# A state-space mixer's first step: loads in order of need, late step sizes, one chunk split on another engine

## The reference

```
proj = x @ W_in.T                       # 512 + 512 + 32*128 + 32*128 + 32 columns
val, gate, B, C, dt = split(proj)
val  = silu(depthwise_conv4(val) + conv_b)
ld   = softplus(dt + dt_bias) * -exp(A_log)
M    = (C . B per head) * exp(cum(ld)[l] - cum(ld)[m]), l >= m
Y    = M @ val + D * val
out  = (Y * silu(gate)) @ W_out.T
```

## Time and profile before

| what | value |
|---|---|
| median of 3 runs | 813.26 us (808.52 to 814.21) |
| profiled execution | 812.88 us, span 811.1 us |
| TensorE busy | 738.9 us, 91% |
| VectorE, ScalarE, GpSimd busy | 74%, 53%, 46% |
| mean granted TensorE clock | 0.965 of full speed |
| step 0 of the mixer ends, step 1 begins | 57.05 us |

### The profile page before, as it was taken

How to read it: one execution, slowest core, us unless ns; L and a number is a source line. 1 busy time by engine, 2 the same in 40 slices (tenths; PEclk the granted TensorE clock), 3 DMA queues, 4 the chain that set the end, 5 groups by cost and what they waited for, 6 DMA issues and landing times. The chain is left out here.

```text
span 811.1 us, 17004 instructions
## 1 busy us (share of the span) xinstructions
PE 738.9 (91%) x5786; PEld 401.0 (49%) x5791; DVE 598.5 (74%) x1037; ACT 432.8 (53%) x781; POOL 370.0 (46%) x408
## 2 busy tenths in 40 slices
PE   6699999999999999999999999997799998686673
PEld 2355565555655555555555565665134443333342
DVE  4578767687686786776767778885788898449995
ACT  5665445754444664544575544554277887532333
POOL 5466337463453583433749637633023212115672
PEclk9799999999999999999999999999699999798997
DMA  7355421227423132542223533220230000034401
GB/s 262 97 168 169 104 51 54 65 50 126 134 52 87 43 78 52 168 103 49 54 58 84 98 72 67 62 45 1 95 112 22 21 22 21 0 127 167 151 26 52
DMA packets 35509, 66.28 MB, mean 82 GB/s; under 512 B 7121, under 2 KB 12113, under 8 KB 33873
## 3 DMA queue, kind: packets, MB, share of 16 engines
q1 hardware_dynamic: 34896, 65.28, 30.0%
q10 hardware_dynamic: 576, 0.56, 0.2%
HBM read 62.49 MB, written 2.42 MB: 80 GB/s over the span
## 5 line engine op out<-in xcount | busy, mean ns | idle before, releaser
L280 POOL TENSOR_TENSOR cum_rows<-cum_rows,cum_t 128x512 f32<-128x512 f32 x128 | 136.4, 1076 | 195.4 <-DMA cum_rows<-cum_scratch 195.4
L758 PE MATMUL pring<-xt_hi,w_hi 128*128 (+1 forms) x576 | 173.5, 383 | 11.5 <-DVE conv_h L647 6.8
L758 PE MATMUL pring<-xt_lo,w_hi 128*128 (+1 forms) x576 | 172.8, 382 | 0.0
L758 PE MATMUL pring<-xt_hi,w_lo 128*128 (+1 forms) x576 | 172.7, 382 | 0.0
L626 DVE TENSOR_TENSOR bt<-pring,bt 128x512 f16<-128x512 f32 x128 | 88.1, 688 | 74.1 <-ACT bt L434 74.0
L434 ACT CAST bt<-pring 128x512 f16<-128x512 f32 x128 | 74.6, 583 | 116.8 <-PE pring L758 116.8
L630 DVE TENSOR_TENSOR ct<-pring,ct 128x512 f16<-128x512 f32 x128 | 88.2, 689 | 55.6 <-ACT ct L438 55.3
L797 PEld LDWEIGHTS pscore<-ct,bt 128*128 128x128 f16 x1536 | 95.9, 98 | 34.7 <-issue 7.2
L797 PE MATMUL pscore<-ct,bt 128*128 128x128 f16 x1536 | 106.7, 219 | 2.9 <-DVE mt L598 2.2
L438 ACT CAST ct<-pring 128x512 f16<-128x512 f32 x128 | 74.8, 584 | 54.8 <-PE pring L758 54.8
L1089 DVE TENSOR_REDUCE mx<-bank_at 128x4 f32<-128x512 f32 x128 | 83.5, 689 | 14.0 <-PE bank_at L1165 13.0
(11 more groups left out here) (154 smaller groups left out, 944.2 us busy)
## 6 DMA issues: line engine op xcount, KB each, us to landing
cum_rows<-cum_scratch SPq DMA_DIRECT2D x32, 1024.0 KB, 8.0
w_raw<-in_w_in SPq DMA_DIRECT2D x34, 256.0 KB, 7.1
weight_b<-weight_scratch SPq DMA_DIRECT2D x8, 1024.0 KB, 6.5
q_rows<-in_xt SPq DMA_DIRECT2D x4, 512.0 KB, 6.1
acc<-in_x SPq DMA_DIRECT2D x1, 2048.0 KB, 7.6
vals<-in_vals SPq DMA_DIRECT2D x16, 128.0 KB, 2.0
out<-acc SPq DMA_DIRECT2D x4, 512.0 KB, 2.9
w_raw_e<-in_w_up SPq DMA_DIRECT2D x1, 1024.0 KB, 4.8
```

The lines of the kernel that those rows point to most:

```text
L280: nc.gpsimd.tensor_tensor(rows[:, par, :, q], rows[:, par, :, q], own, ALU.subtract).then_inc(sem("since"), 1)
L758: mm = nc.tensor.matmul(bank[name][:], w[:, c, k, cols], x[:, k, bass.ds(n % TB, 1), :].rearrange("p o n -> p (o n)"), start=(i == 0), sto ...
```

## The change

The first step alone is reordered, on all engines; the arithmetic stays the same.

- **Loads.** SyncE issues x block 0, chunks 1 and 2, `ident`, chunk 3, x block 1, chunk 4; then it waits for the running sum of block 0, stores it, issues the two row loads, and behind these chunks 5 and 6, x block 2, chunks 7 and 8, x block 3, `dskip` and `wo`. The load of `acc` waits for the second row load, and the store of the other three sums comes behind it. ScalarE's queue has wdt, chunk 0, dtb, cw. `in_dtb` now counts dtb and cw, `in_wo` counts `dskip` and `wo`, and all waiters want both.
- **Chunk 0.** ScalarE makes only the high part; the low part is one VectorE operation.
- **Softplus** of blocks 1 to 3, and their dt products, go from before slot 0 to slot 4 (TensorE after `turn_values`, ScalarE after `evac_c(0, 4)`).
- **x's blocks.** Blocks 1 to 3 are split on GpSimd: block 1 between chunks 2 and 3, block 2 behind the eight exponents of step 0, block 3 behind those of step 1. TensorE's step 1 is taken out of the loop, and waits for blocks 2 and 3 stand behind it.
- **VectorE** computes the low part and the taps' scaling before the step sizes; the scaling of `dskip` stands behind `low_c(0, 1)`.

```diff
 @block.sync
-            for t in range(TB):
-                sp.dma_start(xt_raw[:, t], io["xt"][:, t]).then_inc(sem(f"in_xt{t}"), 16)
-            for t, name in ((cw, "cw"), (dskip, "dskip"), (ident, "ident")):
-                sp.dma_start(t[:], io[name]).then_inc(sem("in_early"), 16)
-            for c in range(2, CHUNKS):
-                load_chunk(c)
-            sp.dma_start(wo, io["wo"]).then_inc(sem("in_wo"), 16)
+            load_x(0)
+            load_chunk(1)
+            load_chunk(2)
+            sp.dma_start(ident[:], io["ident"]).then_inc(sem("in_ident"), 16)
+            load_chunk(3)
+            load_x(1)
+            load_chunk(4)
...
             for par in range(2):
                 load_rows(0, par, par)
+            load_chunk(5)
+            load_chunk(6)
+            load_x(2)
+            load_chunk(7)
+            load_chunk(8)
+            load_x(3)
+            sp.dma_start(dskip[:], io["dskip"]).then_inc(sem("in_wo"), 16)
+            sp.dma_start(wo, io["wo"]).then_inc(sem("in_wo"), 16)
+            sp.wait_ge(sem("rows1"), 16)
+            sp.dma_start(acc[:], io["x"]).then_inc(sem("in_x"), 16)
+            sp.dma_start(expo[:], io["expo"]).then_inc(sem("in_x"), 16)
             sp.wait_ge(sem("dt_cum"), TB)
             store_sums(1, TB)
-            sp.dma_start(acc[:], io["x"]).then_inc(sem("in_x"), 16)
-            sp.dma_start(expo[:], io["expo"]).then_inc(sem("in_x"), 16)
 @block.gpsimd
-            lo_part(0, 0)
+            pool.wait_ge(sem("w_ready"), 1)
             lo_part(0, 1)
-            split_x(2)
-            split_x(3)
             lo_part(0, 2)
+            split_x(1)
             lo_part(0, 3)
             lo_part(0, 4)
...
+            split_x(2)
+            pool.wait_ge(sem("cum_t"), 2)
             exponents(1, 0)
+            exponents(1, 1)
+            split_x(3)
 @block.scalar
             act.dma_start(wdt[:], io["wdt"]).then_inc(sem("in_wdt"), 16)
+            act.dma_start(w_raw[:, 0], io["w_in"][0, :, 0]).then_inc(chunk_loaded(0), 16)
             act.dma_start(dtb[:], io["dtb"]).then_inc(sem("in_dtb"), 16)
+            act.dma_start(cw[:], io["cw"]).then_inc(sem("in_dtb"), 16)
...
             split_x(0)
             hi_part(0, 0, True)
-            hi_part(0, 1, True)
+            act.wait_ge(sem("in_dtb"), 32)
+            nc.scalar.activation(rate[:, 0:1], dtb[:, 1:2], ACT.Exp).then_inc(sem("rate"), 1)
             act.wait_ge(sem("dt_mm"), 1)
             softplus(slice(0, L), 0)
-            split_x(1)
+            hi_part(0, 1, True)
             hi_part(0, 2, True)
...
+                tanh_gate(0)
+                evac_b(0, 0)
+                tanh_val(0)
+                hi_part(0, 3, True)
+                evac_c(0, 0)
+                hi_part(0, 4, True)
+                evac_b(0, 1)
+                evac_c(0, 1)
+                hi_part(0, 5, True)
+                evac_b(0, 2)
+                evac_c(0, 2)
+                decays(0, 0)
+                hi_part(0, 6, True)
...
+                evac_c(0, 4)
+                act.wait_ge(sem("dt_mm"), TB)
+                softplus(slice(L, TOK), 3)
+                evac_b(0, 5)
+                hi_part(0, 8, True)
+                evac_c(0, 5)
+                decays(0, 4)
 @block.vector
             split_x(0)
+            dve.wait_ge(sem("w_hi"), 1)
+            nc.vector.scalar_tensor_tensor(out=w_lo[:, 0], in0=w_raw[:, 0], scalar=W_SCALE, in1=w_hi[:, 0], op0=ALU.mult, op1=ALU.subtract).then_inc(sem("w_ready"), 1)
+            dve.wait_ge(sem("in_dtb"), 32)
...
                 low_c(0, 1)
+                dve.wait_ge(sem("in_wo"), 32)
+                nc.vector.tensor_scalar(dskip[:], dskip[:], W_SCALE * W_SCALE, None, ALU.mult).then_inc(sem("cw_half"), 1)
                 low_b(0, 2)
 @block.tensor
...
                 scores(0, 2)
                 turn_values(0)
+                for t in range(1, TB):
+                    step_widths(t)
                 for s in range(4, SLOTS):
```

More of the change, by code:

```diff
@@ L324, in refill @@
                     lo_part(g + 1, c)
-            with pool.Fori(1, TB - 1) as n:
-                exponents(n, 1)
-                exponents(n + 1, 0)
             refill(0)
@@ L397, in hi_part @@
                         act.wait_ge(sem("c_proj"), (TB * g - 1) * SLOTS + c)
+                if first and c == 0:
+                    nc.scalar.mul(w_hi[:, c], w_raw[:, c], W_SCALE).then_inc(sem("w_hi"), 1)
+                    return
                 nc.scalar.mul(w_hi[:, c], w_raw[:, c], W_SCALE)
                 nc.scalar.mul(w_raw[:, c], w_raw[:, c], W_SCALE).then_inc(sem("w_hi"), 1)
-            act.wait_ge(sem("in_dtb"), 16)
-            nc.scalar.activation(rate[:, 0:1], dtb[:, 1:2], ACT.Exp).then_inc(sem("rate"), 1)
             def softplus(s, done):
@@ L452, in first_step @@
             def first_step():
[L454 to L460, removed]
+                tanh_gate(0)
[11 more added lines that the diff above has]
+                hi_part(0, 6, True)
                 evac_b(0, 3)
-                decays(0, 0)
+                decays(0, 1)
                 evac_c(0, 3)
-                decays(0, 1)
-                hi_part(0, 6, True)
                 decays(0, 2)
+                hi_part(0, 7, True)
                 evac_b(0, 4)
@@ L469, in first_step @@
                 evac_c(0, 4)
-                hi_part(0, 7, True)
+                act.wait_ge(sem("dt_mm"), TB)
[3 more added lines that the diff above has]
+                evac_c(0, 5)
                 decays(0, 4)
-                evac_b(0, 5)
-                evac_c(0, 5)
+                evac_b(0, 6)
                 decays(0, 5)
[L475 to L480, removed]
+                evac_c(0, 6)
+                decays(0, 6)
+                act.wait_ge(sem("in_wo"), 32)
                 nc.scalar.copy(wo_parts[:, 0], wo).then_inc(sem("wo_hi"), 1)
+                evac_b(0, 7)
+                evac_c(0, 7)
+                decays(0, 7)
             def step(n, refill=None, queries=()):
-                silus(n)
+                tanh_gate(n)
+                tanh_val(n)
                 if refill is not None:
@@ L581, in _ @@
             sums(0)
[L582 to L586, removed]
+            dve.wait_ge(sem("cw_half"), 2)
             dve.wait_ge(sem("zeroed"), 1)
@@ L688, in first_step @@
                 low_c(0, 3)
-                sums(3)
                 weigh(0, 2)
                 pad_values(0)
[L692 to L697, removed]
+                low_b(0, 4)
+                low_c(0, 4)
+                weigh(0, 3)
+                step_sizes(slice(L, TOK), 3)
+                low_b(0, 5)
+                rates(slice(L, TOK), 3)
+                sums(1)
+                sums(2)
+                sums(3)
+                low_c(0, 5)
+                weigh(0, 4)
+                low_b(0, 6)
+                low_c(0, 6)
+                weigh(0, 5)
+                low_b(0, 7)
+                low_c(0, 7)
+                weigh(0, 6)
+                sums_turned(1, TB)
+                dve.wait_ge(sem("cw_half"), 3)
             def step(n, norm=False):
@@ L765, in warm, with step_widths @@
                                  start=True, stop=True)
[L767 to L771, removed]
+            def step_widths(t):
                 pe.wait_ge(sem(f"in_xt{t}"), 16)
@@ L888, in _ @@
             first_step()
-            with pe.Fori(1, STEPS - 2) as n:
+            step(1)
+            pe.wait_ge(sem("xt_late"), 6)
+            with pe.Fori(2, STEPS - 2) as n:
                 step(n)
```

46 lines of the change are left out of this document (24 added, 22 removed).

## The result

| | before | change |
|---|---|---|
| median of 20 runs each | 813.65 us (808.52 to 815.38) | 815.62 us (813.08 to 818.0) |
| ratio, 95% interval | | 1.0031 (1.0019 to 1.0044) |
| profiled execution, span | 812.88, 811.1 | 815.23, 813.4 |
| running sum of block 0 | 16.9 | 10.4 |
| TensorE's longest wait in step 0 | 5.62, ends 23.19 | 13.07, ends 35.32 |

The change is slower by 0.3%, a difference that 20 runs tell from none. Forecast were 811.5 us, 1.4 under the profiled execution; the sign was wrong, and the time lies in the range.

A forecast was written before the change was run, and what follows sets the result against it. TensorE, without gaps over 0.2 us from 42.56 us on, was taken as the bound. Of 5.7 us gained early 2.2 stay at slot 4; less 0.5 for softplus and 0.25 in step 1, 1.4 off 812.88: 811.5, range 804.5 to 817.5.

The forecast's parts named there:

- the landing of `wo`: First step's loads: wo, queued behind the rows, lands at 30.9 to 33.5 us, taken as 31.5.
- step 1: Second mixer step: its rows land 4.4 us into it, costing 0 to 1 us, taken as 0.25.
- rival (c): First step: loads behind the rows slow both row loads by 2.6 us each, wo near 36.3, 816.3 us; chance 0.2.
- The early chain: Start of the first step: val at 7.8 us, running sum at 11.2 instead of 16.9, a gain of 5.7 us.
- The new wait: First step: VectorE waits for wo, so TensorE stops at about 22 us, idles for 11, and B3 starts at 33.1.
- The rate: Loads queued behind the rows: 2.5 MB at 414 GB/s, 6.4 us until wo lands.
- The slow pair: TensorE's B3 pair after the wait: 4.4 us at the lowered clock against 2.6 at the full clock.
- Slot 4: First step: slot 4 starts at 40.4 us instead of 42.56, leaving 2.2 of the 5.7 us.
- Softplus in slot 4: First step, slot 4 on: moved softplus and scans cost 0.5 us, so the next step starts at 55.4 instead of 57.05.
- The slack of 1.2 us: Second mixer step in the kernel before: the first decays had about 1.2 us of slack.
- Steps behind step 1: Mixer loop: each further step lasts as long as before; the forecast is wrong as a whole if they change.
- Rival (b): First step: loads behind the rows run ahead of them, B3 at 28.6, a gain of 5.9 us, 807.0 us; chance 0.18.

The follow-up runs named there:

- e7: The change with all loads first, dskip's scaling at the step's end, softplus in slot 1, but chunk 0 as in the kernel before: 802.79 us, 0.9886 to before.
- e1: The change with VectorE's wait for dskip and wo and the scaling of dskip moved to the end of its first step: 810.94 us, 0.9982 to before.
- e3: The change with the eight loads behind the row loads issued only once the second row load has landed: 815.65 us, 1.0034 to before.
- e5: The change with chunks 5 to 8 ahead of the running-sum wait, dskip's scaling behind slot 5's weighing, softplus one copy later, its dt products after slot 4's scores: 798.39 us.
- e2: The change with all loads of the first step ahead of the wait for the running sum, the row loads behind them: 804.54 us, 0.9896 to before.

## Why the prediction was wrong

Two terms of the sum failed: the landing of `wo` (31.5 forecast, 33.66 measured) and step 1 (0.25 forecast, 2.8 measured). The case that came true is rival (c), to which I had given 0.2, in a smaller form. That its 816.3 us lies near the measured time is luck: it has step 1 start 1.9 us too late, misses 2.5 us in step 1, and gives nothing back at the end, where the profile gave 1.7.

- **The early chain** was right: running sum said for 11.2, came at 10.4. Val started at 9.37, not 7.8, behind the warming matmuls; nobody paid for it, for the tables' chain ended where the convolution needed it, and e7, where val came no later either, finds no price in chunk 0.
- **The new wait, its mechanism,** was right: VectorE idle for `wo` (forecast from about 20 until 31.5; measured 19.7 to 33.66), TensorE stopped at about 22 as said, B3 held up; e1 shows that it was this wait.
- **The landing of `wo`, the term that failed first.** I took 31.5, "near the lower end, as the bytes are the same and only their mixture costs". It was 33.66: the rows came at 27.1 for 24.5, which is rival (c) with 3.0 us (e3) instead of 5.2 (the second row load alone is stretched, not both), and the sum lies past the 33 from which (c) was to decide. As long as VectorE's wait stands there, each us here moves B3 by one. The rate was sound: from the rows' landing to `wo` it took 6.6 us for my 6.4. (387 GB/s is not the lowest microsecond of the first loads, as I wrote: from 3 to 4 us they moved 339, and from 9 to 10 341.)
- **The slow pair** was 5.03 us for 4.4. The clock, in the stretches with the columns of the earlier trace rows:
```profile
26.00:27.00 1.00, 0.00 (x0) 0.00 (x0) 0.00 (x0) 0.00 (x0) 0.00 (x0) 0.81 1.03 381
27.00:28.00 1.00, 0.00 (x0) 0.00 (x0) 0.00 (x0) 0.00 (x0) 0.00 (x0) 0.50 1.04 402
...
40.00:41.00 1.00, 1.00 (x14) 0.79 (x13) 0.01 (x1) 0.45 (x1) 0.00 (x0) 0.86 0.00 0
```
After TensorE stopped at 22.2 it was granted the lower level, 1.2 GHz, from 27 until 40: the whole pair ran at it, while the row at 27.12 that I took my 4.4 from had part of it behind. Behind this stop of 13 us the pair cost 2.4 us over the 2.6 at 2.4 GHz.
- **Slot 4** therefore began at 43.01, forecast 40.4: +2.2 by `wo`, +0.6 by the pair, -0.3 by the dt products (1.52 for 1.78) and roundings. The gain of 2.2 that the forecast had left was gone here.
- **Softplus in slot 4**, 0.5 forecast, cost 0.8 (15.27 us to step 1 for 14.5; 0.61 of it is the wait ahead of the scores at 54.02). Its price on ScalarE was as costed. In ScalarE's rows the table load follows the operation ahead of it by 0.02 us (46.91, 0.52, then 47.45) and the next follows the load by 0.01 (47.45, 1.28, 48.74), so the drain of about 1.38 us that the Trainium skill states (ScalarE: Activation LUTs, "What ACT_TABLE_LOAD costs") shows here as little as before.
- **"Step 1", 0.25 forecast, was 2.8: the second term that failed, and the larger.** Said was that the rows are issued near 52 and land 4.4 us into the step. The store went out at 53.36; store to issue took 3.56 us (before 3.42, 44.11 to 47.53; I had taken 2, from the first store's 1.57), and issue to use 9.2 instead of 7.8: 7.9 us into the step. Of the 3.5 us more than 4.4, the store's place is 0.5, store to issue 1.6 and issue to use 1.4. Why the last two are longer here than for the first rows was not tested. The slack of 1.2 us was right, so 3 us of lateness were to be paid in full, as the table above shows.
- **Sum:** forecast -1.4 at step 2, measured +4.04: 2.6 by slot 4, 0.3 in slots 4 to 7, 2.5 in step 1. Behind step 2 the profile gave back 1.7, on which I had counted nothing, and the profiled time came 3.7 us above the forecast.
- Steps behind step 1 kept their length, as forecast. Rival (b), the loads overtaking, was wrong: landings followed issues.

## What to carry to other kernels

Loads put behind an urgent one in the same queue were not free here, even those that are needed later: count both their own lateness and what they add to the urgent one, and look in each engine's list for the smallest operation that waits for the last of them. When a chain is brought forward, price the first thing that now lies behind it, and put ahead of it whatever is needed before the next stretch, as e5 does. A store and reload of a moved result takes its whole distance again: take store to issue and issue to use from the instance that you move, not from the fastest one in the trace.

## What the hardware showed beside that

- A repeated row load (1 MB out of few KB) is slow in itself: a pair took 11.8 to 12.2 us with nothing behind (e2, e3), 172 to 178 GB/s; ordinary loads moved 402 GB/s in the microsecond from 27 to 28. Behind such a pair SyncE's issues take about 1 to 2 us each (2.13 for two, 1.98 for `dskip`, 1.06 for `wo`), against 0.4 when the rows had landed (e3: 0.82 for two).
- Two operations of VectorE on 128 columns, 2.27 and 1.14 us beside a GpSimd subtraction, took 0.35 and 0.42 with GpSimd idle (9.60, 9.98 above); `val_t` at 15.52 took 1.19 beside another (0.68 at 31.13 in the kernel before, with GpSimd idle), while operations that read PSUM kept 0.68 beside it. Before, the scaling of the taps, on 16 columns, was stretched as well, ahead of the convolution; it takes 0.17 with GpSimd idle. The prediction did not count it among the causes of the late convolution, and the change moves it out of the way too. Before, then the change:
```profile
16.81 2.03 DVE L583 TENSOR_SCALAR cw<-cw 128x16 f32<-128x16 f32 x1
```
```profile
7.49 0.17 DVE L604 TENSOR_SCALAR cw<-cw 128x16 f32<-128x16 f32 x1
```
The Trainium skill, GPSIMD Engine Reference, "Key points", says that the two engines contend when VectorE's instruction has two inputs in SBUF (or runs in a 2-port performance mode), without a size. The stretched operations on 128 and 512 columns agree with the first; whether the scaling of the taps, with one input and a constant, is a case of the second no run here shows.
